# A batch loop written out, the first value products of the fifteenth head ahead, and one tile of the next values ahead of the last denominators

## The chip, the cores and the metric

The kernel runs on one core of one Trainium2 chip. The metric is the device time of one execution in microseconds (us). Names: TensorE (PE; its weight loads are PEld), VectorE (DVE), ScalarE (ACT), GpSimd (POOL) and SyncE (SP), which here only issues DMAs.

## The reference, cut to what matters

The program computes four layers on x of shape (4, 1024, 256), each added to x: a recurrent layer, a mixture of 8 experts, causal attention with 16 heads, and a mixture of 32 experts. The change is in the attention:

```
q = einsum('qdh,bcd->bhcq', Q, x) * sq ;  k = ... K ... ;  v = ... V ... * sv
att = einsum('bhcq,bhCq->bhcC', q, k) / d_query
att = where(causal, att, -inf)
p = softmax(att, axis=-1)
y = einsum('bhcC,bhCv->bhcv', p, v)
z = einsum('dvh,bhcv->bcd', W, y) * (sqrt(d_embed / d_value) / num_heads)
```

B = 4 batches of S = 1024 rows, 16 heads of width 64, all in fp32 (products of split high and low parts where precision needs it). x here is the layernorm of the residual.

## The kernel before, in words

Every engine has its own program, written out by hand in the order in which it is to run. Engines meet at semaphores only. There is no scheduler: what stands first in an engine's list runs first, and whoever waits holds up all that stands behind it.

The attention stage goes batch by batch, and in a batch head by head (`head_products` on TensorE, `head_steps` on VectorE, `head_exps` on ScalarE, `head_adds` on GpSimd, `head_operands` on SyncE). A batch is a call of `batch_products`, `batch_steps`, `batch_exps`, `batch_adds`, `batch_operands`. Batch 0 and batch 3 are called with plain numbers and so are straight code. Batches 1 and 2 are the two rounds of a loop (`Fori(0, B - 2)`) on each of the five engines; in it, the numbers that semaphores are waited for depend on the round and are computed in registers.

What TensorE does in a head, in short names:
- M4 to M11 (`scores`, L2439): scores of the next head from which VectorE takes row maxima (L1828 and L1835). N0 to N3 are the same for the head after that.
- L2462 and L2463 (`scores_t`), with a mask product L2470: the transposed scores of this head, blocks 0 to 11. ScalarE takes exp of each (L1259) into c_p.
- `outputs_of(0)`, `(1)`, `(2)` (L2491): the products of c_p with the head's values, in three rounds of four blocks. The first round is 14 matmuls.
- `denominators` (L2500): sums of c_den over rows for the head before, after which VectorE inverts (L1840), SyncE sends the result to DRAM and back over all partitions (L707, L710), and VectorE multiplies y with it (L1847).
- projections (L2426), the transposed maxima (L2446, one a head), and for a pair of heads the output product `z_of` (L2518).

M, N, X, Z, T and V products share two PSUM banks, taken in turn ("turn over" 0 and 1): each waits until the user of its bank two places before it in the list has been read out.

In the fifteenth head (index 14) of a batch with a successor (`fetch`), TensorE also transposes the next batch's x (`transpose_x`, L2396: units X0, X1 and later X2, X3, 8 matmuls for two units). ScalarE copies them out as c_xT_hi (L1211), then VectorE writes the rest as c_xT_lo (L1798), and only this frees the bank. M7 comes right behind X0 and X1 and uses X0's bank.

At the end of the batch stand the denominators of the last head (they wait for ScalarE to copy y, L1241, and for GpSimd's sums), then 8 tiles of the next batch's values (`values`, L2403, 6 matmuls each, copied out by ScalarE at L1218), the last z products, which need y multiplied with its inverses, and 8 more tiles.

Of the kernel before, what the change touches and what calls it, by code (L numbers as in the profile page):

```python
# [45 lines left out]
def network(nc, x_in, a_params, w12T, w3T, gate0T, wqkT, wvT, woT, swT, bias1, ewT, out):  # L46
    B, S, D = x_in.shape
# [20 lines left out]
    QT = S // P  # L68
# [17 lines left out]
    with ExitStack() as ctx:  # L86
# [514 lines left out]

        LATE = {4 + 5 * n: EARLY + n for n in range(NG - EARLY)}
        ZERO_PARTS = 4
        BATCH_STEPS = 91
        GP = 2 * S // GT
        LO_DVE = 6

# [1 line left out]
        def _(sp):  # L609
# [138 lines left out]
            def batch_operands(b, route, nxt):  # L748

                tables = batch_turns(b, route, nxt)  # L750
                sp.wait_ge(s_cve, b * 2 + 1)
                stage_v(0, 0)
                sp.wait_ge(s_cve, b * 2 + 2)
                sp.sem_inc(s_pass, 1)
                for hp in range(NPAIR):
                    for h in range(2):
                        head_operands(b, hp, h, nxt, route, tables)
                if nxt:
                    spread_inverses(b * NH + (NH - 1), 1)
# [13 lines left out]
            stage_weights(2, 0, False)  # L773
            stage_max(0, 0, first_turns()["T"])
            batch_operands(0, False, True)
            with sp.Fori(0, B - 2) as i:
                batch_operands(i + 1, True, True)
            batch_operands(B - 1, True, False)

            for h in range(2):  # L780
                sp.wait_ge(s_cw[h], NPAIR * 16 + (B - 1) * NPAIR * 32)
# [39 lines left out]
        def _(pool):  # L821
            st = Steps(pool, s_pool)
# [137 lines left out]
            def batch_adds(b, route, nxt):  # L960
                for hd in range(NH):
                    head_adds(b, hd, nxt, route)
# [6 lines left out]
            pool.wait_ge(s_cset, 3)  # L969
            copy_k(0, 0)  # L970
            batch_adds(0, False, True)
            with pool.Fori(0, B - 2) as i:
                batch_adds(i + 1, True, True)
            batch_adds(B - 1, True, False)
            finish_stage(pool, 2)

            for n in range(2):
# [23 lines left out]
        def _(act):  # L1001
# [373 lines left out]
            for m in range(STB):  # L1375
                probabilities(0, 0, m)
            batch_exps(0, False, True)
            with act.Fori(0, B - 2) as i:
                batch_exps(i + 1, True, True)
            batch_exps(B - 1, True, False)  # L1380

            leave_stage(act)

# [92 lines left out]
        def _(dve):  # L1476
# [627 lines left out]
            for n in range(4):  # L2104
                maximum(1, n, first_turns(), "N")
            batch_steps(0, False, True)
            with dve.Fori(0, B - 2) as i:
                st.loop(i, B - 2, BATCH_STEPS)
                batch_steps(i + 1, True, True)
                st.end()  # L2110
            batch_steps(B - 1, True, False)
            def shared_gate(g):

                dve.wait_ge(s_dst, g + 1)
# [89 lines left out]
        def _(pe):  # L2204
# [199 lines left out]
                                        start=(n == 0 and k == 0), stop=(n == 2 and k == KD - 1))  # L2404
                ins.then_inc(s_cv, 1)

            def values(batch, a, table):

                for t in range(QT):
                    r, turn = table[f"V{a * QT + t}"]  # L2410
                    pe.wait_ge(s_turn[r], turn)
                    value_tile(2 + r, a, t)
# [137 lines left out]
            def head_products(b, hp, h, nxt, route, tables):  # L2550
                hd = hp * 2 + h
                pair = b * NPAIR + hp
                H = b * NH + hd
                fetch = nxt and hd == NH - 2
                follows, more, zs = nxt or hd + 1 < NH, nxt or hd + 2 < NH, hd >= 2
                table = tables[hd]

                def maxima(*chunks):
                    for n in chunks * follows:
                        scores(H + 1, 1 - h, n, table[f"M{n}"])  # L2560

                def maxima_ahead(*chunks):
                    for n in chunks * more:
                        scores(H + 2, h, n, table[f"N{n}"])

                def projections(*steps):
                    for n in steps * more:
                        project(H + 2, pair + 1, h, n)

                def z_units(*units):  # L2570
                    for n in units * zs:
                        z_of(pair - 1, 1 - hp % 2, n, table[f"Z{n}"])

                def outputs_of(r):
                    for m in range(r * ROUND, (r + 1) * ROUND):
                        c, j = BLOCKS[m]
                        if j == 0:

                            pe.wait_ge(s_cyn, H * (2 * NC2) + (2 * c + 2))
                            if c and hd:  # L2580
                                pe.wait_ge(s_cr, H)
                        outputs(H, pair, h, m)

                scores_t(H, h, 3)
                mask_t(3)
                maxima(4)
                scores_t(H, h, 4)
                maxima(5)
                scores_t(H, h, 5)
                maxima(6)  # L2590
                if fetch:
                    transpose_x(b + 1, 0, table)
                    maxima(7)
                    denominators(H - 1, 1 - h)
                    maxima(8)
                else:
                    projections(0)
                    maxima(7)
                    if hd:
                        denominators(H - 1, 1 - h)  # L2600
                    projections(1)
                    if h == 1:
                        z_units(2, 3)
                    projections(2)
                    maxima(8)
                outputs_of(0)

                scores_t(H, h, 6)
                maxima(9)
                scores_t(H, h, 7)  # L2610
                maxima(10)
                scores_t(H, h, 8)
                mask_t(8)
                maxima(11)
                if fetch:
                    transpose_x(b + 1, 1, table)
                    projections(0, 1, 2)
                outputs_of(1)
                if follows:
                    transpose_max(H + 1, table)  # L2620
                for m in (9, 10, 11):
                    scores_t(H, h, m)
                mask_t(9, 10, 11)
                if fetch:

                    for k in range(KD):
                        r, turn = table[f"X{KD + k}"]
                        pe.wait_ge(s_turn[r], turn + 1)
                projections(3, 4)
                maxima_ahead(0)  # L2630
                projections(5)
                maxima_ahead(1)
                maxima_ahead(2)
                if follows:
                    scores_t(H + 1, 1 - h, 0)
                maxima_ahead(3)
                if follows:
                    for m in (1, 2):
                        scores_t(H + 1, 1 - h, m)
                    mask_t(0, 1, 2)  # L2640
                outputs_of(2)
                if h == 0 and zs:

                    pe.wait_ge(s_cym, pair)
                    z_units(0, 1)
                if route:
                    for n, a in enumerate(ROUTE_AT):
                        g = b * 2 + (n - 2)
                        if hd == a:
                            transpose_rows3(g, n, table)  # L2650
                        if hd == a + 1:
                            for k in range(KD):
                                r, turn = tables[a][f"U{k}"]
                                pe.wait_ge(s_turn[r], turn + 1)
                            r, turn = table["U2"]
                            pe.wait_ge(s_turn[r], turn)
                            expert_logits(r_xT, 2 + r).then_inc(s_dsc, 1)
                        if hd == a + 3:
                            r, turn = table["U3"]
                            pe.wait_ge(s_turn[r], turn)  # L2660
                            count_before3(g, 2 + r)

            def batch_products(b, route, nxt):
                tables = batch_turns(b, route, nxt)
                for hp in range(NPAIR):
                    for h in range(2):
                        head_products(b, hp, h, nxt, route, tables)
                pair = b * NPAIR + (NPAIR - 1)
                table = tables[NH]
                denominators(b * NH + (NH - 1), 1)  # L2670
                if nxt:
                    values(b + 1, 0, table)
                    pe.wait_ge(s_cym, pair + 1)
                else:
                    spread_on_chip(b * NH + (NH - 1))
                for n in range(QT // 2):
                    if not nxt and n % 2 == 0:
                        pe.wait_ge(s_cym, pair + (1 + n // 2))
                    z_of(pair, 1, n, table[f"Z{n}"])
                if nxt:  # L2680
                    values(b + 1, 1, table)
# [49 lines left out]
            mask_t(0, 1, 2)  # L2731
            pe.wait_ge(s_dcast, 3)
            batch_products(0, False, True)
            with pe.Fori(0, B - 2) as i:
                batch_products(i + 1, True, True)
            batch_products(B - 1, True, False)

            pe.wait_ge(s_cks, B * NH * 4)
            leave_stage(pe)
# [169 lines left out]
```

## Time and profile before

| | us |
|---|---|
| timed runs, median of 3 | 2199.08 (2198.98 to 2201.33) |
| profiled execution, its own time | 2198.34 |
| its span, first to last instruction | 2196.1 |
| attention stage, batch 0 to batch 3 | about 646 to 1944 |
| TensorE busy over the span | 1923.5 (88%) |
| mean granted clock of TensorE | 0.935 |

A clock of 1.00 is the upper of TensorE's two levels (2.4 GHz), 0.50 the lower (1.2 GHz). Times in the rows count from the start of the span. In the attention stage batch 0 ends at about 983.5, batch 1 at 1317, batch 2 at 1652. In a row of the timeline the bracket says how long the engine had been idle before it and whose work ended the wait.

### The profile page before, as it was taken

The numbers are of one execution on the slowest core, as the hardware profiler recorded it, in microseconds if no ns is written. First come the engines' busy times: TensorE is split into PE (matmuls) and PEld (weight loads), VectorE is DVE, ScalarE is ACT, GpSimd is POOL, SyncE is SP. The second block draws the span as 40 slices with busy tenths as digits, with TensorE's granted clock in tenths as the row PEclk, the third lists the DMA queues.
The fourth block names the chain that finished last, engine by engine and source line by source line (L and its number), as shares of the span: only waits on it lengthen the run. The fifth ranks groups of instructions, "written<-read, shape, count | busy, mean of one in ns | idle before, by whom it ended". The sixth has DMA issues, their size and how long they took to land. (4 is left out here: it accounts for less than half of the span.)

```text
span 2196.1 us, 42575 instructions
## 1 busy us (share of the span) xinstructions
PE 1923.5 (88%) x11815; PEld 1444.0 (66%) x11816; DVE 1361.8 (62%) x3638; ACT 1079.2 (49%) x2250; POOL 1175.1 (54%) x1159
## 2 busy tenths in 40 slices
PE   4852999999689999999999999999999999974870
PEld 2541788888567677677777677777677777752660
DVE  6765343443367777656777656777656877653763
ACT  5321334333355555646655546555646565521760
POOL 3455233232216665536587735577845677835782
PEclk8765999999889999999999999999999999986995
DMA  9652533333331211211121101121101121121979
GB/s 337 213 204 83 125 51 51 51 51 53 79 91 50 56 51 48 54 32 53 50 75 44 48 24 53 50 57 48 45 28 52 47 59 46 39 94 53 205 132 255
DMA packets 215710, 177.59 MB, mean 81 GB/s; under 512 B 85442, under 2 KB 200727, under 8 KB 214880
## 3 DMA queue, kind: packets, MB, share of 16 engines
q1 hardware_dynamic: 177904, 138.78, 21.5%
q0 software_dynamic: 28656, 27.61, 8.3%
q10 hardware_dynamic: 8960, 8.92, 1.2%
q8 instruction: 88, 1.44, 0.3%
q14 instruction: 102, 0.84, 0.1%
HBM read 95.05 MB, written 80.72 MB: 80 GB/s over the span
## 5 line engine op out<-in xcount | busy, mean ns | idle before, releaser
L950 POOL TENSOR_TENSOR c_den_late<-c_den_late,c_p 128x512 f32<-128x512 f32 (+3 forms) x384 | 408.9, 1065 | 247.6 <-ACT c_p L1259 203.6
L1259 ACT ACTIVATE c_p<-PS 128x512 f32<-128x512 f32 (+3 forms) x768 | 342.9, 491 | 230.1 <-PE PS L2470 128.6
L2491 PE MATMUL PS<-c_p,c_vh 128*64 128x256 f32 (+1 forms) x2816 | 322.0, 349 | 0.0
L2439 PE MATMUL PS<-c_k,c_q 128*128 128x512 f32 (+2 forms) x768 | 288.2, 376 | 16.3 <-DVE c_max L1828 5.2
L2462 PE MATMUL PS<-c_q,c_k 128*128 128x512 f32 (+2 forms) x768 | 287.4, 378 | 4.1 <-issue 1.8
L2491 PEld LDWEIGHTS PS<-c_p,c_vh 128*64 128x64 f32 x2816 | 204.5, 137 | 102.5 <-issue 39.7
L886 POOL DMA_INDIRECT acc<-b_y,b_tok x71 | 110.5, 1557 | 277.6 <-ACT b_y L1129 242.9
L2463 PE MATMUL PS<-c_q,c_k 128*128 128x512 f32 (+2 forms) x768 | 258.9, 348 | 0.0
L1250 ACT ACTIVATE c_q<-PS 64x512 fp32r<-64x512 f32 x256 | 151.3, 591 | 205.3 <-PE PS L2426 178.4
L1835 DVE CUSTOM_DVE_ANT_0 PS<-PS,c_maskq,c_max 128x128 f32<-128x128 f32 (+3 forms) x256 | 143.0, 559 | 126.1 <-PE PS L2439 90.8
L1828 DVE TENSOR_REDUCE c_max<-PS 128x1 f32<-128x512 f32 x256 | 175.0, 684 | 55.1 <-PE PS L2439 52.5
L950 POOL TENSOR_TENSOR c_den<-c_den,c_p 128x384 f32<-128x384 f32 (+2 forms) x192 | 141.3, 736 | 120.1 <-ACT c_p L1259 94.8
L2439 PEld LDWEIGHTS PS<-c_k,c_q 128*128 128x128 f32 x768 | 145.6, 190 | 89.4 <-DVE c_max L1835 29.2
L1835 DVE CUSTOM_DVE_ANT_0 PS<-PS,c_maskq 128x128 f32<-128x128 f32 (+3 forms) x256 | 125.9, 501 | 113.8 <-PE PS L2439 101.8
L2462 PEld LDWEIGHTS PS<-c_q,c_k 128*128 128x128 f32 x768 | 145.0, 189 | 33.1 <-issue 15.8
L919 POOL DMA_INDIRECT routed<-r_rows,r_slot x128 | 129.3, 1010 | 61.4 <-DVEq L1946 33.6
L1716 DVE SCALAR_TENSOR_TENSOR b_hid<-b_sg,PS 128x512 f32<-128x512 f32 x71 | 48.8, 688 | 177.4 <-issue 129.6
L2463 PEld LDWEIGHTS PS<-c_q,c_k 128*128 128x128 f32 x768 | 145.3, 189 | 8.8
L2347 PE MATMUL PS<-b_w3T,b_hT 128*128 x568 | 134.7, 380 | 2.0 <-ACT b_hT L1120 1.1
L2330 PE MATMUL PS<-b_w12h,b_tT_hi 128*128 x284 | 129.0, 454 | 5.5 <-DVE b_tT_lo L1709 5.5
L2518 PE MATMUL PS<-c_wo,c_yT 128*128 128x256 f32 x512 | 124.6, 387 | 0.0
L990 POOL DMA_INDIRECT acc<-d_y,d_tok x64 | 100.2, 1566 | 40.7 <-ACT d_y L1439 22.6
(304 smaller groups left out, 4008.8 us busy)
## 6 DMA issues: line engine op xcount, KB each, us to landing
c_vh<-c_v SPq DMA_DIRECT2D x64, 256.0 KB
c_rrow<-rden SPq DMA_DIRECT2D x63, 256.0 KB, 3.7
routed<-b_empty SPq DMA_DIRECT2D x32, 289.0 KB, 9.5
d_xe<-routed SPq DMA_DIRECT2D x32, 289.0 KB
b_xt<-routed SPq DMA_DIRECT2D x71, 130.0 KB
b_w12T<-in_w12T_dram SPq DMA_DIRECT2D x16, 512.0 KB, 13.3
d_acc<-acc SPq DMA_DIRECT2D x16, 512.0 KB, 8.7
c_st_hi<-wqk_split SPq DMA_DIRECT2D x48, 128.0 KB
```

Source lines behind the costliest of these rows:

```text
L919: pool.indirect_dma_start(routed1, bass.IndirectOffsetOnAxis(ap=r_slot[n][:, j // K1, j % K1:j % K1 + 1], axis=0), r_rows[n][:, j // K1, : ...
L950: pool.tensor_tensor(den[:, off:], den[:, off:], p, ALU.add).then_inc(s_cPa, 1)
L1250: act.activation(dst, src, ACT.Copy).then_inc(s_cqs, 1)
L1259: act.activation(c_p[:, P_AT[h][m]:P_AT[h][m] + WIDTH[m]], PS[:, ST_BANK[m % STB], skip:skip + WIDTH[m]], ACT.Exp, scale=ATT_SCALE).then_i ...
L1828: dve.tensor_reduce(dst, src, AX_X, ALU.max).then_inc(s_turn[bank], 1)
L1835: dve.tensor_tensor_reduce(src, src, c_maskq[:, 512 - w:512], 1.0, dst if c else BIG, ALU.add, ALU.max, dst).then_inc(s_turn[bank], 1)
L2330: pe.matmul(PS[:, 2 * j + c, :], b_tT[0][:, j, k, :], b_w12h[k][:, cols], start=(k == 0), stop=False)
L2347: ins = pe.matmul(PS[:, 6 + j, 0:D], b_hT[:, j, k, :], b_w3T[:, k, bass.ds(e * D, D)], start=(k == 0), stop=(k == KH - 1))
L2439: pe.matmul(PS[:, 2 + use[0], 0:max(w, 256)], c_q1[h][:, t * P:(t + 1) * P], c_k1[h][:, c * 512:c * 512 + max(w, 256)], start=True, stop=T ...
L2462: pe.matmul(PS[:, bank, 0:n], c_k1[h][:, j * P:(j + 1) * P], c_q1[h][:, q], start=True, stop=False)
L2463: ins = pe.matmul(PS[:, bank, 0:n], c_k2[h][:, j * P:(j + 1) * P], c_q2[h][:, q], start=False, stop=not diagonal)
L2491: ins = pe.matmul(dst, c_vh[h][:, j, :], moving, start=(j == 0), stop=(t0 == 2 + a))
```

## The change

Three edits.

1. On all five engines the loop over batches 1 and 2 is gone; the batches are written out with plain numbers. `BATCH_STEPS`, a count that the loop on VectorE needed, goes.
2. In the fifteenth head, `outputs_of(0)` stands ahead of M7, right behind the transposes X0 and X1, instead of behind M8. In all other heads it stays where it was.
3. At the end of a batch, one of the eight value tiles is issued ahead of the denominators.

```
-            with pe.Fori(0, B - 2) as i:
-                batch_products(i + 1, True, True)
-            batch_products(B - 1, True, False)
+            for b in range(1, B):
+                batch_products(b, True, b < B - 1)
...
-            def values(batch, a, table):
+            def values(batch, a, table, tiles=range(QT)):
-                for t in range(QT):
+                for t in tiles:
...
                 if fetch:
                     transpose_x(b + 1, 0, table)
+                    outputs_of(0)
                     maxima(7)
                     denominators(H - 1, 1 - h)
                     maxima(8)
...
                     maxima(8)
-                outputs_of(0)
+                    outputs_of(0)
...
+                if nxt:
+                    values(b + 1, 0, table, range(1))
                 denominators(b * NH + (NH - 1), 1)
                 if nxt:
-                    values(b + 1, 0, table)
+                    values(b + 1, 0, table, range(1, QT))
                     pe.wait_ge(s_cym, pair + 1)
```

The same loop edit stands on SyncE, GpSimd, ScalarE and VectorE. Lines behind the first edit have smaller numbers after it: L2439 becomes L2432, L2491 L2484, L2500 L2493, L2403 and L2396 become L2396 and L2389.

TensorE, fifteenth head of batch 0, before: xn is the layernormed x, the rows of 128x256 and 128x512 from c_k and c_q behind it are M7 and M8, c_pick marks the denominators, c_vh the value products.

```order
L2396 MATMUL PS<-ident,xn_172 128x128 [waits c_turn_over0]
L2396 MATMUL PS<-ident,xn_172 128x128 x3
L2439 MATMUL PS<-c_k_1_142,c_q_1_140 128x256 [waits c_turn_over1]
L2500 MATMUL PS<-c_den_152,c_pick 32x128 [waits c_y_taken,c_probs_added]
L2500 MATMUL PS<-c_den_152,c_pick 32x128 x3
L2500 MATMUL PS<-c_den_late,c_pick 32x128 x4
L2439 MATMUL PS<-c_k_1_142,c_q_1_140 128x512 [waits c_turn_over0]
L2491 MATMUL PS<-c_p,c_vh_148 64x256 [waits c_probs_ready,c_head_v_staged0,c_y_taken]
```

The same place after:

```order
L2389 MATMUL PS<-ident,xn_172 128x128 [waits c_turn_over0]
L2389 MATMUL PS<-ident,xn_172 128x128 x3
L2484 MATMUL PS<-c_p,c_vh_148 64x256 [waits c_probs_ready,c_head_v_staged0,c_y_taken]
L2484 MATMUL PS<-c_p,c_vh_148 64x256
L2484 MATMUL PS<-c_p,c_vh_148 64x128 [waits c_probs_ready]
L2484 MATMUL PS<-c_p,c_vh_148 64x256
L2484 MATMUL PS<-c_p,c_vh_148 64x128 [waits c_probs_ready]
L2484 MATMUL PS<-c_p,c_vh_148 64x128
L2484 MATMUL PS<-c_p,c_vh_148 64x128 [waits c_probs_ready]
L2432 MATMUL PS<-c_k_1_142,c_q_1_140 128x256 [waits c_turn_over1]
L2493 MATMUL PS<-c_den_152,c_pick 32x128 [waits c_y_taken,c_probs_added]
```

The value products moved ahead of M7 (the wait on turn over 1) and of the denominators; each row of them stands for one block or half of one.

TensorE, end of batch 0, after: the last value products of the sixteenth head, the tile of the next values (c_wv, c_xT), the denominators, the second tile.

```order
L2484 MATMUL PS<-c_p,c_vh_149 64x128 [waits c_probs_ready]
L2396 MATMUL PS<-c_wv_hi,c_xT_hi 128x512 [waits c_turn_over0]
L2396 MATMUL PS<-c_wv_hi,c_xT_hi 128x512
L2396 MATMUL PS<-c_wv_hi,c_xT_lo 128x512 x2
L2396 MATMUL PS<-c_wv_lo,c_xT_hi 128x512 x2
L2493 MATMUL PS<-c_den_152,c_pick 32x128 [waits c_y_taken,c_probs_added]
L2493 MATMUL PS<-c_den_152,c_pick 32x128 x3
L2493 MATMUL PS<-c_den_late,c_pick 32x128 x4
L2396 MATMUL PS<-c_wv_hi,c_xT_hi 128x512 [waits c_turn_over1]
```

Before, the three rows of the denominators stand directly behind the value products, and all tiles behind them.

TensorE, end of the loop's body, before: the last tile of values, the register step and the branch that closes a round, and then the code of batch 3.

```order
L2403 MATMUL PS<-c_wv_lo,c_xT_hi 128x512 x2
L2411 REGISTER_ALU
L2403 MATMUL PS<-c_wv_hi,c_xT_hi 128x512 [waits c_turn_over1]
L2403 MATMUL PS<-c_wv_hi,c_xT_hi 128x512
L2403 MATMUL PS<-c_wv_hi,c_xT_lo 128x512 x2
L2403 MATMUL PS<-c_wv_lo,c_xT_hi 128x512 x2
L2734 REGISTER_ALU
L2734 COMPARE_AND_BRANCH
L2462 MATMUL PS<-c_q_0_139,c_k_0_141 128x256 [waits c_probs_ready]
```

The end of batch 1 after:

```order
L2396 MATMUL PS<-c_wv_hi,c_xT_hi 128x512 [waits c_turn_over1]
L2396 MATMUL PS<-c_wv_hi,c_xT_hi 128x512
L2396 MATMUL PS<-c_wv_hi,c_xT_lo 128x512 x2
L2396 MATMUL PS<-c_wv_lo,c_xT_hi 128x512 x2
L2455 MATMUL PS<-c_q_0_139,c_k_0_141 128x256 [waits c_probs_ready]
L2456 MATMUL PS<-c_q_0_143,c_k_0_145 128x256
```

The branch and the register steps between products are gone; the next batch's first transposed scores follow directly.

## Rows read from the trace of the kernel before

**Rows 1.** Windows, batch 1 (from:to, length, busy us of PE, PEld, DVE, ACT, POOL, PEclk, DMA).
```profile
983.50:1319.30 335.80, 329.44 (x2190) 242.12 (x2189) 228.66 (x551) 191.70 (x411) 215.53 (x224) 0.99 0.18 50
```
**Rows 2.** Timeline of TensorE, fifteenth head of batch 0 (start us, us, what, idle before).
```profile
916.82 1.25 PE L2396 MATMUL PS<-ident,xn 128*128 128x128 f32 x8 [0.19 <-DVE c_max L1835]
919.58 0.38 PE L2439 MATMUL PS<-c_k,c_q 128*128 128x256 f32 x1 [1.51 <-DVE c_xT_lo L1798]
...
920.90 1.52 PE L2491 MATMUL PS<-c_p,c_vh 128*64 128x256 f32 x14
922.35 0.50 PE L2462 MATMUL PS<-c_q,c_k 128*128 128x512 f32 x1
```
**Rows 3.** Timeline of TensorE, M7 in the fifteenth head of batches 1 and 2.
```profile
1250.33 0.58 PE L2439 MATMUL PS<-c_k,c_q 128*128 128x256 f32 x1 [1.65 <-DVE c_xT_lo L1798]
...
1586.71 0.38 PE L2439 MATMUL PS<-c_k,c_q 128*128 128x256 f32 x1 [1.64 <-DVE c_xT_lo L1798]
```
**Rows 4.** Timeline of VectorE, maximum M9 of the same head, batch 0.
```profile
923.48 0.62 DVE L1835 CUSTOM_DVE_ANT_0 PS<-PS,c_maskq,c_max 128x384 f32<-128x384 f32 x1 [1.36 <-PE PS L2439]
```
**Rows 5.** Timeline of TensorE: X3 in that head, which waits for M11's maximum.
```profile
925.86 0.66 PE L2396 MATMUL PS<-ident,xn 128*128 128x128 f32 x4 [0.39 <-DVE c_max L1835]
```
**Rows 6.** Windows round the waits of Rows 3, columns as in Rows 1.
```profile
1247.00:1250.00 3.00, 1.55 (x10) 0.84 (x8) 1.39 (x4) 2.93 (x7) 2.65 (x5) 1.00 0.56 148
1250.00:1257.00 7.00, 6.67 (x36) 4.51 (x37) 2.93 (x6) 0.45 (x2) 2.91 (x3) 0.51 0.09 16
...
1585.00:1592.00 7.00, 5.36 (x37) 3.67 (x37) 3.19 (x6) 1.56 (x4) 4.26 (x5) 0.76 0.06 14
```
**Rows 7.** Timeline of TensorE: the denominators at the end of batches 0, 1, 2.
```profile
957.15 0.42 PE L2500 MATMUL PS<-c_den,c_pick 128*32 128x128 f32 x8 [0.96 <-ACT c_yT L1241]
...
1291.03 0.43 PE L2500 MATMUL PS<-c_den,c_pick 128*32 128x128 f32 x8 [0.87 <-ACT c_yT L1241]
...
1626.04 0.42 PE L2500 MATMUL PS<-c_den,c_pick 128*32 128x128 f32 x8 [0.87 <-ACT c_yT L1241]
```
**Rows 8.** Timeline of ScalarE: one of the value tiles copied out.
```profile
1294.66 0.60 ACT L1218 ACTIVATE c_v<-PS 128x512 f32<-128x512 f32 x1 [0.76 <-PE PS L2403]
```
**Rows 9.** Timeline, end of batch 0: y multiplied on VectorE, then its z product.
```profile
964.56 1.23 DVE L1847 TENSOR_TENSOR c_yT<-c_yT,c_rrow 128x1024 f32<-128x1024 f32 x1 [5.75 <-DMA c_rrow<-rden]
...
968.78 1.55 PE L2518 MATMUL PS<-c_wo,c_yT 128*128 128x256 f32 x6
```
**Rows 10.** Timeline of TensorE: end of the loop's first round, end of its second.
```profile
1316.92 0.61 PE L2403 MATMUL PS<-c_wv_lo,c_xT_hi 128*128 128x512 f32 x2
1319.30 0.38 PE L2462 MATMUL PS<-c_q,c_k 128*128 128x256 f32 x1 [1.76 <-issue]
...
1651.95 0.62 PE L2403 MATMUL PS<-c_wv_lo,c_xT_hi 128*128 128x512 f32 x2
1652.40 0.28 PE L2462 MATMUL PS<-c_q,c_k 128*128 128x256 f32 x1
```
**Rows 11.** Timeline of TensorE: transposed maxima, first and fourteenth head, batches 1, 2, 3.
```profile
992.92 0.27 PE L2446 MATMUL PS<-ident,c_max 128*8 128x128 f32 x1
...
1238.66 0.27 PE L2446 MATMUL PS<-ident,c_max 128*8 128x128 f32 x1
...
1328.79 0.27 PE L2446 MATMUL PS<-ident,c_max 128*8 128x128 f32 x1
...
1575.06 0.27 PE L2446 MATMUL PS<-ident,c_max 128*8 128x128 f32 x1
...
1661.80 0.27 PE L2446 MATMUL PS<-ident,c_max 128*8 128x128 f32 x1
...
1906.06 0.27 PE L2446 MATMUL PS<-ident,c_max 128*8 128x128 f32 x1
```
**Rows 12.** DMA queues, instruction fetches: window 1319:1652 (batch 2), then 1653:1943 (batch 3).
```profile
q8 instruction: 21, 0.34, 0.4%
...
q8 instruction: 16, 0.26, 0.4%
```

More of the change, by code:

```diff
@@ L603, in network @@
         ZERO_PARTS = 4
-        BATCH_STEPS = 91
         GP = 2 * S // GT
@@ L775, in _ @@
             batch_operands(0, False, True)
-            with sp.Fori(0, B - 2) as i:
-                batch_operands(i + 1, True, True)
-            batch_operands(B - 1, True, False)
+            for b in range(1, B):
+                batch_operands(b, True, b < B - 1)
             for h in range(2):
@@ L971, in _ @@
             batch_adds(0, False, True)
-            with pool.Fori(0, B - 2) as i:
-                batch_adds(i + 1, True, True)
-            batch_adds(B - 1, True, False)
+            for b in range(1, B):
+                batch_adds(b, True, b < B - 1)
             finish_stage(pool, 2)
@@ L1377, in _ @@
             batch_exps(0, False, True)
-            with act.Fori(0, B - 2) as i:
-                batch_exps(i + 1, True, True)
-            batch_exps(B - 1, True, False)
+            for b in range(1, B):
+                batch_exps(b, True, b < B - 1)
             leave_stage(act)
@@ L2106, in _ @@
             batch_steps(0, False, True)
[L2107 to L2111, printed above, removed]
+            for b in range(1, B):
+                batch_steps(b, True, b < B - 1)
             def shared_gate(g):
@@ L2733, in _ @@
             batch_products(0, False, True)
-            with pe.Fori(0, B - 2) as i:
-                batch_products(i + 1, True, True)
-            batch_products(B - 1, True, False)
+            for b in range(1, B):
+                batch_products(b, True, b < B - 1)
             pe.wait_ge(s_cks, B * NH * 4)
```

## The prediction, made before the changed kernel was run

> **What bounds the kernel now.** I read the page first: TensorE is busy for 88% of the span, more than any other engine. Then the windows by batch: in batch 1 it is busy for 329.4 of 335.8 us [rows 1], while VectorE, ScalarE and GpSimd are busy for 229, 192 and 216. So between 646 and 1944 us the time is TensorE's list of work plus the few places where it stands still or runs slowly. The change adds no product to TensorE and takes none away; it can gain only in those places. I looked for them in the list of waits of TensorE and then in its timeline, in the fifteenth head, at the end of a batch and at the closing of the loop. The stage behind the attention starts when TensorE and the rest have left it, so I take what is gained here as gained at the end.
>
> **First value products ahead in the fifteenth head.** M7 may not write its bank before VectorE has taken the low part of x from it. In batch 0 TensorE waits 1.51 us there [rows 2], in batches 1 and 2 1.65 and 1.64 us [rows 3]. Ahead of M7 the changed list puts 14 value products, which take 922.35 - 920.90 = 1.45 us [rows 2]. Their inputs are there: they need the probabilities of blocks 0 to 3, which ScalarE has finished before it takes x, and the head's values, which were sent for a head earlier. So 1.45 us of the wait are filled and 0.06 to 0.2 us stay. Everything behind M8 comes 1.45 us earlier, if VectorE follows. It does its part of the head in its own order; it stood idle for 1.36 us before the maximum of M9 because TensorE came late [rows 4], and that idle time is what lets it follow. Behind it X3 waits 0.39 us for the maximum of M11 [rows 5], and that wait may grow by 0.1. I take 1.35 to 1.4 us in each of three heads, together 4.2 us. Bounds: 0, if VectorE were the limit up to X3, and 1.5 in each, the whole wait; I am near the upper end because the idle row of VectorE is nearly as long as the move.
>
> **The clock behind that wait.** In batch 1 the granted clock is 0.51 in the seven us behind the wait, in batch 2 0.76 [rows 6]; that is the lower level (1.2 GHz) for all or half of the stretch. Before it fell, TensorE was at work for only 1.55 of 3.00 us [rows 6]. The work lost is 7 x (1 - 0.51) = 3.4 us and 7 x (1 - 0.76) = 1.7 us, 5.1 us together; in batch 0 the same wait did not lower the clock. With 0.2 us of the wait left, TensorE is nearly dense there. I take all 5.1 us. Bounds: 0 (the clock falls anyway, for the small waits before the transposes too) and 5.1.
> The Trainium skill, "TensorE: Matmul & The Clock Gate" (Part 1), has the full clock lost after an idle stretch and given back by a busy one. Here the engine was half busy before the clock fell, so the trace does not agree with idleness as the condition. If the rule held to the letter, the fall would have another cause than this wait, the 5.1 us would stay lost, and the sum would be 5.1 smaller; that is the first rival.
>
> **One value tile ahead of the last denominators.** The denominators wait for ScalarE to copy y: 0.96, 0.87 and 0.87 us [rows 7], and nothing stands ready behind them on TensorE because it takes its list in order. A tile takes 0.60 + 0.76 = 1.36 us of TensorE, by the pace at which ScalarE gets tiles [rows 8]. It is longer than the wait, so the wait goes: 2.7 us. The denominators come 0.4 to 0.5 us later in the list's own time. Behind them are VectorE's inversion, SyncE's two transfers and the multiplication of y, which ends at 964.56 + 1.23 = 965.79; TensorE needs it at 968.78 [rows 9]. Of these 2.99 us, 0.96 go because TensorE arrives earlier and 0.4 because the chain starts later; 1.6 us stay, so no new wait. ScalarE copies y first and the tile then, as before. Bounds: 0 and 2.9.
>
> **The loop written out: its closing.** From the last tile of batch 1 to the first product of batch 2 it is 1319.30 - 1316.92 = 2.38 us, with 1.76 us in which TensorE waits for nothing that the profile shows. From batch 2 to batch 3, without a branch back, it is 1652.40 - 1651.95 = 0.45 us [rows 10]. I take 1.9 us. It is paid once: two rounds have one branch back. Other engines branch back too, but each does so while TensorE works on its tiles. Bounds: 1.5 and 2.4.
> The Trainium skill, "Runtime: NRT & Kernel Launch" (Instruction fetch mechanics), says that a taken branch out of the fetched pages stops the engine until the target's page is there, and that straight code is fetched ahead. The two closings above agree; by that rule the gain is the same 1.9.
>
> **The loop written out: its registers.** In the loop each wait with a number of its own is preceded by register steps; in straight code there are none. From the first to the fourteenth head's transposed maximum batch 1 takes 1238.66 - 992.92 = 245.74 us, batch 2 246.27, batch 3, straight and with the same routing work, 244.26 [rows 11]. The differences are 1.48 and 2.01, together 3.49. Half a microsecond in batch 2 is a wait for a DMA that may come again, and batch 3 does not make the next x in its thirteenth head. I take 2.8 us. Bounds: 0 (all of it from these other causes) and 4.5 (the two last heads gain as well).
>
> **Sum.** 4.2 + 5.1 + 2.7 + 1.9 + 2.8 = 16.7 us. The profiled execution took 2198.34 us (2.2 outside the span of 2196.1), so 2181.6 us. The median of the timed runs is 0.7 us above the profiled one, so 2182.4 us, 0.76% less. Nothing is charged for the written-out code: its fetches run ahead on their own queue. The one cost is the later denominators, hidden as shown.
>
> **Rivals.**
> First, the clock is not won back: it falls in the fifteenth heads for what is left of the waits, or it falls elsewhere, where waits now lie differently in time. Batch 0 speaks for that being open, since the same wait left the clock at its upper level there; against it, the waits themselves shrink from 1.6 to 0.2 us. Time: 2182.4 + 5.1 = 2187.5 us.
> Second, only the loop edits count, and the moved products are given back: VectorE is late for M11 and X3, and the later chain of inverses holds the z products. For it speaks that VectorE's list in this head has hardly other idle time; against it the 1.6 us of slack. Without 4.2, 5.1 and 2.7 the gain is 4.7: 2194.4 us, at the edge of what can be told from no change.
> Third, slower: the supply of instructions. In batches 1 and 2 TensorE's code would now be new code all the way, and if each fetch stopped it as the branch back did, it would pay. Window rows show 16 fetches on the larger instruction queue in straight batch 3 and 21 in batch 2 [rows 12]. With 16 in each of two batches at 1.9 us this is 61 us, and the time 2182.4 + 61 = 2243 us; from nine such stops on (17 us) the kernel is no faster. Against it: straight batch 3 is the fastest of all in the same work, and the loop's second round fetches its code again, more than straight code does, so writing it out adds no traffic.
> Fourth, more is won than I count: the upper bounds of the waits and the registers give about 3 us more, 2179 us.
>
> **How the numbers follow.** The forecast (2179 to 2186) 0.62; the clock not won back, wholly or in part (2186 to 2191) 0.20; only the loop edits 0.06; slower 0.04; more than counted (below 2179) 0.08. Two per thousand are 4.4 us, about what a measurement of this kernel can tell from no change. Faster by more than that is below 2194.7 us: forecast, first and fourth rival and half of the second, 0.92. Within it 0.04, slower 0.04. The range is 2177 to 2190 us: at the low end it has some of the fourth rival and the shift of the last stage's own clock by chance, at the high end the clock rival.
>
> **What would show it.** In the changed profile: M7's wait in the three fifteenth heads at 0.3 us or less; no granted clock under 0.9 within them; X3's wait under 0.6 us; the fifteenth head 20.2 us long in all three batches, from one transposed maximum to the next. The denominators at a batch's end without a wait, the z products still without one. From batch 1's last tile to the next product 0.45 us. From first to fourteenth head 244.3 to 244.8 us in batches 1 and 2. Wrong would be the forecast if the clock falls in batches 1 or 2, if the last stage behind 1944 us takes longer by what was won, or if TensorE waits for nothing visible in the written-out batches.

## The result and the profile after

| | before | changed |
|---|---|---|
| timed runs, median | 2199.03 us (2198.98 to 2201.33, 4 runs) | 2180.3 us (2178.95 to 2182.31, 4 runs) |
| ratio of the changed kernel to before, 95% interval | | 0.9923, 0.9911 to 0.9935 |
| profiled execution, span | 2196.1 us | 2179.1 us |

The kernel became 18.7 us faster; 16.7 had been forecast. Two later comparisons, on two different chips, gave ratios of 0.9931 (0.9918 to 0.9944) and 0.9927 (0.9910 to 0.9944), some 15 to 16 us; the medians there lie 15.2 and 13.8 us apart.

The page of the changed kernel, its line of busy times and its line of the granted clock:

```profile
PE 1915.9 (88%) x11815; PEld 1437.9 (66%) x11816; DVE 1360.6 (62%) x3638; ACT 1078.8 (50%) x2250; POOL 1176.0 (54%) x1159
...
PEclk8765999999889999999999999999999999986995
```

TensorE's list has as many products as before (11815), and they were busy for 7.6 us less, though nothing is left out. From batch 0's first transposed maximum to the last of all it was 5.9 us less (1237.54 and 1231.61), while the time between those two points shrank by 15.0 us; so some 9 us of the gain is idle time that went, and the rest is products that took less time. A product is recorded as longer at the lower clock (M7 0.58 us in batch 1 [rows 3], 0.38 in batch 0 [rows 2]), so part of the rest is clock.

TensorE in the fifteenth head of batch 0 (start us, us, what, idle before), against [rows 2, 5]:

```profile
913.82 1.26 PE L2389 MATMUL PS<-ident,xn 128*128 128x128 f32 x8 [0.18 <-DVE c_max L1831]
915.01 1.52 PE L2484 MATMUL PS<-c_p,c_vh 128*64 128x256 f32 x14
916.59 0.38 PE L2432 MATMUL PS<-c_k,c_q 128*128 128x256 f32 x1
...
921.62 0.66 PE L2389 MATMUL PS<-ident,xn 128*128 128x128 f32 x4 [0.33 <-DVE c_max L1831]
```

The value products stand in the place of the wait, and M7 (916.59) carries no bracket: the wait of 1.51 us is gone. X3 still waits, 0.33 us against 0.39.

VectorE at M9 and M11 of that head (L1831, columns as above), against [rows 4]:

```profile
919.29 0.62 DVE L1831 CUSTOM_DVE_ANT_0 PS<-PS,c_maskq,c_max 128x384 f32<-128x384 f32 x1 [0.17 <-DVE c_max L1824]
...
920.75 0.76 DVE L1831 CUSTOM_DVE_ANT_0 PS<-PS,c_maskq,c_max 128x512 f32<-128x512 f32 x1 [0.23 <-PE PS L2432]
```

Its idle time of 1.36 us before M9 is gone: it now goes from one maximum to the next. It has become the slower of the two at one place. The maximum of M8 and, behind it, M10, which uses M8's bank:

```profile
918.49 0.63 DVE L1824 TENSOR_REDUCE c_max<-PS 128x1 f32<-128x512 f32 x1
...
919.17 0.50 PE L2432 MATMUL PS<-c_k,c_q 128*128 128x512 f32 x1
```

M10 starts when that maximum is done (918.49 + 0.63 = 919.12), 0.49 us behind the product before it in the list; before, it started 0.22 us behind it.

Windows behind the value products of the fifteenth heads of batches 1 and 2 (from:to, length, busy us of PE, PEld, DVE, ACT, POOL, granted clock, DMA share, GB/s), against [rows 6]:

```profile
1246.00:1253.00 7.00, 6.44 (x41) 4.24 (x41) 4.57 (x10) 4.67 (x9) 5.83 (x5) 1.00 0.15 40
...
1574.00:1581.00 7.00, 6.54 (x43) 4.29 (x42) 4.68 (x9) 4.68 (x10) 5.63 (x5) 1.00 0.14 38
```

The granted clock is 1.00 where it was 0.51 and 0.76.

TensorE at the end of batch 0, against [rows 7]; then VectorE's multiplication of y and the z products, against [rows 9]:

```profile
950.44 1.52 PE L2484 MATMUL PS<-c_p,c_vh 128*64 128x256 f32 x14
951.89 0.73 PE L2396 MATMUL PS<-c_wv_hi,c_xT_hi 128*128 128x512 f32 x2
...
953.49 0.43 PE L2493 MATMUL PS<-c_den,c_pick 128*32 128x128 f32 x8
...
961.18 1.22 DVE L1843 TENSOR_TENSOR c_yT<-c_yT,c_rrow 128x1024 f32<-128x1024 f32 x1 [6.03 <-DMA c_rrow<-rden]
...
963.74 3.89 PE L2511 MATMUL PS<-c_wo,c_yT 128*128 128x256 f32 x16
```

The tile follows the value products at once and the denominators (953.49) follow it without a wait. y is ready at 962.40, 1.3 us before it is needed.

TensorE where the loop closed, the end of batch 1, against [rows 10]:

```profile
1304.99 0.62 PE L2396 MATMUL PS<-c_wv_lo,c_xT_hi 128*128 128x512 f32 x2
1305.44 0.28 PE L2455 MATMUL PS<-c_q,c_k 128*128 128x256 f32 x1
```

0.45 us, as between batches 2 and 3 before.

The transposed maxima (now L2439): fourteenth and fifteenth head of batch 0, then first and fourteenth of batches 1, 2 and 3, against [rows 11]:

```profile
905.16 0.27 PE L2439 MATMUL PS<-ident,c_max 128*8 128x128 f32 x1
925.46 0.27 PE L2439 MATMUL PS<-ident,c_max 128*8 128x128 f32 x1
...
987.90 0.27 PE L2439 MATMUL PS<-ident,c_max 128*8 128x128 f32 x1
...
1232.08 0.27 PE L2439 MATMUL PS<-ident,c_max 128*8 128x128 f32 x1
...
1314.86 0.27 PE L2439 MATMUL PS<-ident,c_max 128*8 128x128 f32 x1
...
1559.74 0.27 PE L2439 MATMUL PS<-ident,c_max 128*8 128x128 f32 x1
...
1642.47 0.27 PE L2439 MATMUL PS<-ident,c_max 128*8 128x128 f32 x1
...
1887.07 0.27 PE L2439 MATMUL PS<-ident,c_max 128*8 128x128 f32 x1
```

From first to fourteenth head that is 244.18, 244.88 and 244.60 us, where it was 245.74, 246.27 and 244.26. The larger instruction queue, batch 1 (987:1315), against [rows 12]:

```profile
q8 instruction: 17, 0.28, 0.4%
```

17 fetches where a round of the loop had 21 (18 in batch 2, 1315 to 1642): the written-out code costs no more fetching.

With this ruler, the starts of the 64 transposed maxima, the kernels of this study can be laid beside each other, one profiled execution each. The columns are: from first to fourteenth head (two batches), the fifteenth head (three), and the batch end, from the sixteenth head's transposed maximum to the first of the next batch (three), all in us.

| kernel | batch 1, 2 | fifteenth head, batch 0, 1, 2 | end of batch 0, 1, 2 |
|---|---|---|---|
| before | 245.74, 246.27 | 21.58, 24.82, 23.47 | 43.14, 45.15, 43.12 |
| changed | 244.18, 244.88 | 20.30, 20.32, 20.32 | 42.36, 42.36, 42.33 |
| straight_only | 244.38, 244.73 | 21.54, 23.15, 23.17 | 43.11, 43.11, 43.13 |
| move_only | 245.63, 246.33 | 20.32, 20.66, 20.65 | 43.19, 46.81, 43.10 |
| tile_only | 245.61, 246.53 | 21.60, 24.84, 23.42 | 42.37, 44.53, 42.43 |
| fill_wait | 245.72, 246.29 | 21.57, 21.85, 21.84 | 43.11, 46.77, 43.12 |
| pe_straight | 245.55, 245.63 | 21.56, 24.74, 23.35 | 43.15, 43.45, 43.09 |
| others_straight | 244.85, 245.85 | 21.60, 23.16, 23.23 | 43.08, 45.03, 43.06 |
| three_tiles | 244.27, 244.31 | 20.33, 20.35, 20.33 | 43.67, 43.79, 43.46 |

### The profile page after: what moved, and what is told of

Same layout as the page of the kernel before. It is cut to its first block and busy times, and to the rows that moved or that the text cites. A ratio compares the mean times of both kernels' runs of the same rounds, so it can differ in the third digit from the quotient of the medians.

```text
span 2179.1 us, 39171 instructions
## 1 busy us (share of the span) xinstructions
PE 1915.9 (88%) x11815; PEld 1437.9 (66%) x11816; DVE 1360.6 (62%) x3638; ACT 1078.8 (50%) x2250; POOL 1176.0 (54%) x1159
## 5 line engine op out<-in xcount | busy, mean ns | idle before, releaser
L2484 PE MATMUL PS<-c_p,c_vh 128*64 128x256 f32 (+1 forms) x2816 | 319.4, 347 | 0.0
L2432 PE MATMUL PS<-c_k,c_q 128*128 128x512 f32 (+2 forms) x768 | 288.8, 376 | 11.8 <-DVE c_max L1824 5.2
L2484 PEld LDWEIGHTS PS<-c_p,c_vh 128*64 128x64 f32 x2816 | 202.9, 136 | 101.5 <-issue 38.2
L1831 DVE CUSTOM_DVE_ANT_0 PS<-PS,c_maskq,c_max 128x128 f32<-128x128 f32 (+3 forms) x256 | 143.1, 559 | 116.1 <-PE PS L2432 81.3
L2432 PEld LDWEIGHTS PS<-c_k,c_q 128*128 128x128 f32 x768 | 145.2, 189 | 88.9 <-DVE c_max L1831 33.7
L1831 DVE CUSTOM_DVE_ANT_0 PS<-PS,c_maskq 128x128 f32<-128x128 f32 (+3 forms) x256 | 125.9, 501 | 114.3 <-PE PS L2432 97.3
```

The lines of the kernel that those rows point to most:

```text
L1831: dve.tensor_tensor_reduce(src, src, c_maskq[:, 512 - w:512], 1.0, dst if c else BIG, ALU.add, ALU.max, dst).then_inc(s_turn[bank], 1)
L2432: pe.matmul(PS[:, 2 + use[0], 0:max(w, 256)], c_q1[h][:, t * P:(t + 1) * P], c_k1[h][:, c * 512:c * 512 + max(w, 256)], start=True, stop=T ...
L2484: ins = pe.matmul(dst, c_vh[h][:, j, :], moving, start=(j == 0), stop=(t0 == 2 + a))
```

## The experiments

### The three parts, each alone, and all together

straight_only: before, with the five loops written out.

```
-            with pe.Fori(0, B - 2) as i:
-                batch_products(i + 1, True, True)
-            batch_products(B - 1, True, False)
+            for b in range(1, B):
+                batch_products(b, True, b < B - 1)
```

Expected: 

> Only the batches are written out on all five engines; the order on TensorE is that of before. My theory: the closing of the loop costs 1.9 us and the register steps 2.8 us, so about 2194.4 us (4.7 less than before). M7's waits of 1.5 to 1.65 us and the denominators' waits of 0.9 us stay as they are, and so does the chance that the clock falls in the fifteenth heads. From first to fourteenth transposed maximum batches 1 and 2 take 244.2 to 244.9 us. Rival (all the gain is in the moved products): same as before within 1 us.

Measured: 2186.83 us against 2193.34 of before on that chip, ratio 0.9975 (0.9963 to 0.9986). The closing is 2.0 us shorter (43.11 for 45.15) and the batches are 1.4 and 1.5 us shorter. The waits at M7 stay, and so does a fall of the clock behind them. But the fifteenth head of batch 1 is 1.7 us shorter as well (23.15 for 24.82), which I had not expected: M7's wait there is 1.51 us instead of 1.65, and the lower clock held for about half as long (0.76 in the window below, 0.51 in the one of [rows 6]). That is why the timed gain is 6.5 us and not 4.7. TensorE at M7 in batches 1 and 2:

```profile
1247.91 0.38 PE L2433 MATMUL PS<-c_k,c_q 128*128 128x256 f32 x1 [1.51 <-DVE c_xT_lo L1795]
...
1579.01 0.39 PE L2433 MATMUL PS<-c_k,c_q 128*128 128x256 f32 x1 [1.52 <-DVE c_xT_lo L1795]
```

and windows round the first of them, then the same place of batch 0:

```profile
1244.50:1248.00 3.50, 1.81 (x11) 1.07 (x10) 1.95 (x5) 3.05 (x8) 3.15 (x5) 1.00 0.55 134
1248.00:1255.00 7.00, 6.93 (x45) 4.54 (x46) 3.71 (x9) 1.77 (x3) 3.79 (x4) 0.76 0.10 38
919.00:926.00 7.00, 6.54 (x52) 4.53 (x52) 4.95 (x11) 2.65 (x5) 3.82 (x3) 1.00 0.15 40
```

The clock is 0.76 in the seven us behind the wait in batch 1, and 1.00 in batch 0 behind one as long. Both terms of the theory came in the trace, and the rival, no gain, is out; a third term, part of the clock in batch 1, came with them.

move_only: before, with the move in the fifteenth head alone.

```
                     transpose_x(b + 1, 0, table)
+                    outputs_of(0)
                     maxima(7)
...
-                outputs_of(0)
+                    outputs_of(0)
```

Expected: 

> Only the first value products of the fifteenth head stand ahead of M7; the loop and the tiles stay. My theory: the fifteenth head takes 20.3 us in all three batches (1.3 less in batch 0; 4.5 and 3.2 less in batches 1 and 2 if the clock there fell because of the wait), together 9 us, so about 2190 us. Rival (the clock fell for another reason): 3.9 us less, 2195 us, with a granted clock of 0.5 for some us in a fifteenth head.

Measured: 2188.64 against 2193.34 us, ratio 0.9974 (0.9966 to 0.9983). All three fifteenth heads are short (20.32, 20.66, 20.65) with no lower clock in them, so the fall there did hang on the wait. But the gain is 4.7 us, not 9: the closing of the loop became dearer, 46.81 for 45.15. TensorE at the closing, and a window behind it:

```profile
1310.90 0.38 PE L2462 MATMUL PS<-c_q,c_k 128*128 128x256 f32 x1 [1.93 <-issue]
```
```profile
1311.00:1318.00 7.00, 7.00 (x33) 5.33 (x34) 3.05 (x7) 2.49 (x5) 2.67 (x3) 0.76 0.32 78
```

The clock fell behind the loop's own wait, where it had not fallen before. In the trace the fifteenth heads gave 8.2 us and the closing took 1.7 back; from the first batch's first transposed maximum to the last of all 5.6 us are left, because the untouched part of batch 0 was 0.8 us longer in this execution.

tile_only: before, with the tile ahead alone.

```
+                if nxt:
+                    values(b + 1, 0, table, range(1))
                 denominators(b * NH + (NH - 1), 1)
```

Expected: 

> Only one value tile ahead of the last denominators. My theory: no wait before the denominators at the ends of batches 0, 1, 2, 0.8 us less at each, 2.4 us in all, 2196.7 us. The z products wait for nothing. Rival (the later chain of inverses holds the z products): the wait comes back at the first z product, no gain.

Measured: 2191.61 against 2193.34 us, ratio 0.9992 (0.9981 to 1.0003), no difference in the timed runs. In the trace the batch ends are 0.77, 0.62 and 0.69 us shorter, 2.1 us in all, and the z products wait for nothing. The rival is out by the trace; the timed runs alone could not have told.

after_again: the changed kernel beside its parts.

Expected: 

> The changed kernel once more, on the same chip as its three parts. My theory: the parts add up; its gain over before is the sum of those of the three other kernels of this call (4.7 + 9 + 2.4 = 16 us), 2180 to 2183 us. Rival (the parts overlap or depend on each other): the sum of the three differs from this gain by more than 3 us.

Measured: 2178.17 against 2193.34 us, ratio 0.9931 (0.9918 to 0.9944), 15.2 us. The parts alone sum to 6.5 + 4.7 + 1.7 = 12.9 us, 2.3 less than together. That is within the 3 us that I had set, and the timed runs of before scatter over 2185.57 to 2197.25 there, so the sum alone proves nothing. The traces show that the parts do not add up place by place. In the fifteenth heads straight_only gains 2.0 us and move_only 8.2, the changed kernel 8.9: half of batch 1's fall is counted twice. At the closing straight_only gains 2.0, tile_only 0.6 and move_only loses 1.7, the changed kernel gains 2.8. Each part alone leaves at least one long wait of TensorE in place, at M7 or at the closing, and the clock falls behind one of them.

### Does the clock fall because TensorE stands still?

fill_wait: before, with work of no use in the wait. It adds 12 transposes whose result nobody reads.

```
                     transpose_x(b + 1, 0, table)
+                    for _ in range(12):
+                        pe.transpose(PS[:, 6, 384:512], ident[:, :], ident[:, :])
                     maxima(7)
```

Expected: 

> The kernel before, with 12 transposes of a constant (some 1.3 us, into a part of a bank that nobody reads) between the transposes X0, X1 and M7 of the fifteenth head: work of no use in the wait. My theory (the clock falls because TensorE stands still there): M7 starts when it did before, the fifteenth head takes 21.5 us in batch 0 as before, and 21.6 to 21.8 us in batches 1 and 2 instead of 24.8 and 23.5, with a granted clock of 1.00; a gain of some 4 to 5 us with no useful work moved. Rival (the fall has another cause, such as heat or the place in the program): 23 to 25 us and a clock of 0.5 in one of them, as before.

Measured: fifteenth heads of 21.57, 21.85 and 21.84 us. TensorE from the added transposes to M7 in batch 1, and the window behind:

```profile
1247.42 1.47 PE L2594 MATMUL PS<-ident 128*128 128x128 f32 x12
1249.23 0.39 PE L2439 MATMUL PS<-c_k,c_q 128*128 128x256 f32 x1 [0.33 <-DVE c_xT_lo L1798]
```
```profile
1247.00:1254.00 7.00, 6.67 (x58) 4.96 (x58) 4.01 (x9) 3.12 (x6) 5.08 (x6) 1.00 0.11 30
...
1316.00:1321.00 5.00, 5.00 (x19) 3.71 (x19) 2.56 (x7) 1.75 (x4) 2.66 (x3) 0.66 0.38 95
```

Nothing useful was moved, M7 is still released by the same instruction, and yet the head is 3.0 and 1.6 us shorter in batches 1 and 2, with a clock of 1.00. In batch 0, where the clock had not fallen, nothing changed. So the clock term of the sum belongs to the wait, and it can be won by any work. It is 4.6 us here; what is left between 21.85 or 21.84 and batch 0's 21.57 is the loop's. The timed gain was not what I expected: 2192.25 against 2193.35 us, ratio 0.9996 (0.9985 to 1.0007), no difference. Again the clock fell at the closing instead (0.66 in the second window, 46.77 us for 45.15), which gave 1.6 of the 4.6 us back; for the rest the trace has a gain of 2.7 us over the whole stage, too small for timed runs of this spread.

### Whose registers, whose branch?

pe_straight writes out TensorE's loop alone, others_straight the four other loops alone.

```
pe_straight:      sp, pool, act, dve keep Fori;  pe: for b in range(1, B)
others_straight:  pe keeps Fori;  sp, pool, act, dve: for b in range(1, B)
```

Expected: 

> Only TensorE's batches are written out; the other four engines keep their loops. The closing of the loop (1.9 us) is TensorE's own, so by my theory it goes: 43.1 us from the sixteenth head's transposed maximum to the next instead of 45.2. The 1.4 to 1.5 us a batch that registers cost: if TensorE's own register steps cost them, batches 1 and 2 take 244.4 and 244.7 us from first to fourteenth transposed maximum; rival (the other engines' steps, by late releases): 245.7 and 246.3 as before.

Expected: 

> The other half: SyncE, GpSimd, ScalarE and VectorE written out, TensorE keeps its loop. Theory: the closing of the loop on TensorE stays (45 us), and with TensorE's own register steps as the cause batches 1 and 2 stay at 245.7 and 246.3 us; rival (releases by the others): 244.4 and 244.7.

Measured: 2191.71 us (ratio 0.9993, 0.9978 to 1.0009) and 2190.79 us (0.9990, 0.9978 to 1.0002), against 2193.35; neither can be told from no change by its time. The closing is TensorE's own, nearly all of it: 43.45 us with its loop written out, 45.03 with the others'.

The registers are not TensorE's alone, against my theory, and they do not add up. In batch 1 writing out TensorE is worth 245.74 - 245.55 = 0.2 us, the others 245.74 - 244.85 = 0.9, all together (straight_only) 1.4. In batch 2 it is 0.6, 0.4 and 1.5, but there the kernel before has a wait for a DMA which others_straight also has (0.62 us) and which does not appear in pe_straight and straight_only:

```profile
1406.34 0.49 PE L2462 MATMUL PS<-c_q,c_k 128*128 128x512 f32 x1 [0.49 <-DMA c_q<-c_mr]
```

With that wait taken off it is 0.15, 0.55 and 1.05, so the larger single effect is the other engines' in both batches. The DMA wait itself need not be the loop's: after_again, without any loop, has one of 0.43 us at another place of batch 2. The two halves hide each other: in batch 1, from first to fourteenth head, TensorE is busy for 244.5 us before, 243.8 in pe_straight, 244.0 in others_straight and 243.3 in straight_only, and its waits for VectorE add up to 0.6, 1.0, 0.3 and 0.3 us. Where TensorE alone gets rid of its steps, it waits longer for VectorE. The later releases can be seen at M7 of batches 1 and 2 as well: TensorE waits 1.64 to 1.66 us where the others have loops, and 1.51 or 1.52 where they have none. TensorE at M7 of batch 1 in others_straight:

```profile
1249.04 0.48 PE L2433 MATMUL PS<-c_k,c_q 128*128 128x256 f32 x1 [1.52 <-DVE c_xT_lo L1795]
```

### How near is the chain of inverses?

three_tiles: the changed kernel with three tiles ahead.

```
-                    values(b + 1, 0, table, range(1))
+                    values(b + 1, 0, table, range(3))
```

Expected: 

> The changed kernel with three value tiles ahead of the last denominators instead of one: a dose test of the cost that I called hidden. By the slack of 1.6 us in front of the z products, two more tiles delay the chain of inverses by 2.7 us and make the z products wait 1.1 us at each of three batch ends: 43.5 instead of 42.4 us there, 3.3 us slower than the changed kernel, perhaps with a fall of the clock behind the wait. Rival (the chain is not near the limit): 42.4 us as with one tile.

Measured: 2181.9 against 2193.35 us, ratio 0.9948 (0.9930 to 0.9966), and batch ends of 43.67, 43.79 and 43.46 us. TensorE at the end of batch 0, denominators and z products:

```profile
958.35 0.43 PE L2493 MATMUL PS<-c_den,c_pick 128*32 128x128 f32 x8
...
967.13 3.91 PE L2511 MATMUL PS<-c_wo,c_yT 128*128 128x256 f32 x16 [1.08 <-DVE c_yT L1843]
```

The z products wait 1.08, 1.18 and 0.86 us for y. The expected value was 1.1. One tile is within the slack, three are not; 3.9 us are lost over the three ends against the changed kernel (by the traces; the two were not timed on one chip). Two tiles were not tried. The clock did not fall behind these waits.

### One more move of the same kind

third_round_ahead: the changed kernel, and in the fifteenth head of the last batch the third round of value products ahead of the next head's first scores, where TensorE waits 1.17 us for a DMA.

```
+                if follows and not more:
+                    outputs_of(2)
                 if follows:
                     scores_t(H + 1, 1 - h, 0)
```

Expected: 

> The changed kernel with one more move of the same kind: in the fifteenth head of the last batch, where TensorE waits 1.17 us for the row maxima to come back by DMA before the sixteenth head's first transposed scores, outputs_of(2) (14 value products, 1.45 us) goes ahead of those scores. Theory: the wait is filled except for some 0.2 us (the products themselves wait for the probabilities of blocks 9 to 11, there 1.2 us after they are asked for), 1.1 us less to the last transposed maximum, 14.5 instead of 15.6 us for that head. Rival (GpSimd's sums set the end of the batch): the last denominators wait longer than 2.9 us by just what was gained, and the kernel takes the same time.

Expected: 

> The changed kernel a third time, beside the kernel with one more move, for a comparison on one chip. Theory: fifteenth heads of 20.3 us and batch ends of 42.3 to 42.4 us with no half clock in the batches 1 and 2, 0.7% below before. Rival (the missing falls of the clock were luck): one fall in one of the six places.

Measured: 2182.27 us, and 2183.48 for the changed kernel on the same chip; before 2197.28. Both have a ratio of 0.9927 (0.9911 to 0.9944 and 0.9910 to 0.9944). I had looked for the gain in the wrong interval: the wait stands behind the last transposed maximum, so the 15.6 us before it stayed. TensorE at the last denominators in this kernel, then in the changed kernel (after_third):

```profile
1912.36 0.43 PE L2493 MATMUL PS<-c_den,c_pick 128*32 128x128 f32 x8 [0.44 <-POOL c_den_late L948]
...
1925.98 0.42 PE L2493 MATMUL PS<-c_den,c_pick 128*32 128x128 f32 x8 [3.31 <-POOL c_den_late L948]
```
```profile
1928.21 0.43 PE L2493 MATMUL PS<-c_den,c_pick 128*32 128x128 f32 x8 [2.86 <-POOL c_den_late L948]
```

From the last transposed maximum to these denominators it takes 21.42 us for 21.94. The wait of 1.17 us is gone, and somewhat more than half of it came back, as waits for GpSimd's sums (0.44 at the fifteenth head's denominators, 3.31 for 2.86 at the last). The rival was half right. Half a microsecond is below what the runs can tell; I call this version no faster than the changed kernel. In after_third the six places are again free of the lower clock, as in after_again: fifteenth heads of 20.31, 20.30, 20.32 us.

## Why the prediction was right, point by point

The terms, measured with the ruler in the profiled executions of before and after:

| term | taken | measured | how |
|---|---|---|---|
| value products ahead | 4.2 | 3.8 | 21.58 - 20.30 = 1.28 in batch 0, three times |
| clock behind the wait | 5.1 | 4.6 | (24.82 - 21.85) + (23.47 - 21.84), against the heads of fill_wait |
| tile ahead | 2.7 | 2.4 | 43.14 - 42.36 = 0.78 and 43.12 - 42.33 = 0.79, three ends |
| closing of the loop | 1.9 | 2.0 | 45.15 - 42.36 - 0.79 |
| registers | 2.8 | 3.4 | 1.56 + 1.39 in batches 1 and 2, and 0.5 that is left in their fifteenth heads |
| sum | 16.7 | 16.2 | |

**The move.** VectorE followed as its idle row said, but for one place: M10 waits for the maximum of M8 and follows 0.27 us later than before (0.49 for 0.22), and that is what is missing between 1.28 and the 1.55 us by which the scores behind M8 follow M7 sooner (1.22 for 2.77). The prediction had looked for this loss at X3, whose wait did not grow. The three heads stayed 0.1 us above the 20.2 that it named.

**The clock.** The step that the text called a rival is settled by fill_wait and move_only: the fall hangs on TensorE standing still; that this is not enough by itself, batch 0 shows, where the clock stays up behind the same wait. What I did not see is that the term is not a property of the fifteenth head alone. Take that wait away and leave the loop's closing, and the clock fell there, in both kernels that did so. The changed kernel removes both, and in none of its three profiled executions does the clock fall in the fifteenth heads or at the closings. The step took the whole of 7 x (1 - 0.51) and 7 x (1 - 0.76) as lost time; the heads grew by 4.6 us for it, not 5.1. About 1.7 of the 4.6 would have come from the written-out loop alone (straight_only), which no term of the prediction says. On the Trainium skill's "TensorE: Matmul & The Clock Gate" (Part 1), which names an idle stretch as the condition: TensorE had been busy for 1.81 of 3.50 us in straight_only before the clock fell, so this trace does not agree with idleness as the condition.

**The tile.** 0.78 us came of a wait of 0.96 in batch 0: the tile ahead takes 1.60 us of TensorE (953.49 - 951.89) and not 1.36. The 1.6 us of slack were 1.3, since the chain of inverses starts 0.6 us later and took 0.3 us longer (953.49 to 962.40, before 957.15 to 965.79). three_tiles shows that the slack is real: its waits came out within 0.3 us of the 1.1 expected.

**The loop.** The closing is right in size and in owner. No run separates the branch itself from the fetch of the code behind it. The registers were somewhat larger than taken, because the fifteenth heads gained as well; that was within the bound. My later guess that they were TensorE's own was wrong: the other engines' steps count for more, and only all together give the whole.

**The rivals.** Instruction supply did not matter, 17 fetches and no unexplained wait in the written-out batches. The change did not come back as a loss at the chain of inverses.

**What the sum does not hold.** 17.0 us came between the spans. From the first batch's first transposed maximum to the last of all it is 1258.99 us before and 1243.95 after, 15.0 less (1243.39 and 1242.69 in after_again and after_third); the two untouched stretches, batches 0 and 3 from first to fourteenth head, were 1.3 longer after, by waits that come and go. Ahead of the ruler, in code that is the same, the changed kernel's execution was 4.0 us earlier, and behind it 2.0 us slower. Behind it the twelve profiled executions lie between 271.5 and 277.0 us, whatever the kernel, so this is not the sign of being wrong that the prediction named. So of the forecast's closeness to the timed 18.7 us some is luck, and the two later comparisons lie below it; within the attention stage the terms bear it.

## What to carry to other kernels

Price a wait of the engine that sets the time twice: its length, and what the clock loses behind it, read from the granted clock in the window that follows. When several such waits stand in a program, removing one can hand the fall to another (it did in two of two kernels here), so judge them together, and judge one by its place in the trace, not by the total. Work that is moved ahead of a wait should be no longer than the wait plus the slack of the chain behind it; that slack can be read beforehand and was right to 0.3 us.

## What the runs showed of the hardware that was not expected

- The clock fell in all ten places where TensorE waited 1.51 to 1.66 us at M7 in batches 1 and 2 (five kernels that keep the wait: before, straight_only, tile_only, pe_straight, others_straight), and in none of the five where it waited 1.50 or 1.51 us at M7 in batch 0. In straight_only TensorE's transposes ahead of M7 (1.26 and 1.26 us) and the wait (1.51 and 1.51) are the same in batches 0 and 1, and only batch 1 has the fall. Why batch 0 is spared stays open.
- At the closing, waits of 1.76, 1.90 and 1.70 us (before, tile_only, others_straight) left the clock up, 1.93 and 1.86 us (move_only, fill_wait) brought it down. In the three, it had fallen in the fifteenth head some 65 us before; in the two it had not. No run tells whether that is the reason.
- Unchanged code ahead of the attention stage moved its first transposed maximum between 640.87 and 647.02 us over the twelve profiled executions. That is more than most single edits here are worth, and every timed run holds it.
